# Large weights staged in tiles whose first use is late, and new instruction orders on all engines, in a two-layer attention kernel

## What is computed

```
L0: h  = x + attention(n, n)        n = rmsnorm(x), 16 heads of 16
    h  = h + attention(rmsnorm(h), ctx)
    h  = h + (silu(m @ w_gate) * (m @ w_up)) @ w_down      m = rmsnorm(h), inner 1024
L1: F  = layernorm(h); X = layernorm(ctx)
    a  = attention(F, X, X)          one head of 256, scale 1/16
    c  = gelu(a @ fc1.T + b1) @ fc2.T + b2                 inner 4
    n  = layernorm(c)
    out = F + gamma2 * (c + gamma1 * attention(n, n, n))
```

## Time and profile before

| | us |
|---|---|
| median of 3 runs (1020.12 to 1021.73) | 1021.01 |
| the profiled execution, its own time | 1021.97 |
| its span, first to last instruction | 1020.2 |
| PE busy | 899.7 (88% of the span) |
| DVE busy | 672.6 (66%) |
| ACT busy | 546.0 (54%) |
| POOL busy | 261.6 (26%) |

### The profile page before, as it was taken

How to read it: one execution, slowest core, us unless ns; L and a number is a source line. 1 busy time by engine, 2 the same in 40 slices (tenths; PEclk the granted TensorE clock), 3 DMA queues, 4 the chain that set the end, 5 groups by cost and what they waited for, 6 DMA issues and landing times.

```text
span 1020.2 us, 21920 instructions
## 1 busy us (share of the span) xinstructions
PE 899.7 (88%) x8142; PEld 762.2 (75%) x8142; DVE 672.6 (66%) x1439; ACT 546.0 (54%) x1129; POOL 261.6 (26%) x547
## 2 busy tenths in 40 slices
...
DMA packets 69266, 63.97 MB, mean 63 GB/s; under 512 B 17280, under 2 KB 64496, under 8 KB 69184
## 3 DMA queue, kind: packets, MB, share of 16 engines
q1 hardware_dynamic: 69184, 62.87, 19.3%
...
...
## 4 chain that ended last, share of the span: by engine, by line
PE 77%; DVE 12%; issue 4%; ACT 3%; DMA 2%; POOL 1%; SPq 1%; DVEq 0%; POOLq 0%; ACTq 0%
PE mring L1112 18%; PE ring L1112 17%; PE down_ps L1240 10%; PE od L1207 10%; PE ring L1193 6%; PE ring L1173 6%; DVE mx_sa L959 5%; PE ring L1120 2%; DVE xn_a L932 2%; PE mring L1345 1%; PE mring L1269 1%; PE mring L1316 1%; PE mring L1308 1%; DVE xn_m L932 1%; DVE mx_ca L964 1%
## 5 line engine op out<-in xcount | busy, mean ns | idle before, releaser
L776 ACT ACTIVATE probs<-ring 128x1024 f32<-128x1024 f32 (+1 forms) x192 | 191.8, 1020 | 42.7 <-PE ring L1193 37.5
L559 POOL TENSOR_TENSOR hidT_lo<-hid,hidT_hi 128x256 fp32r<-128x256 f32 x128 | 94.7, 749 | 377.2 <-ACT hidT_hi L799 376.7
L959 DVE TENSOR_REDUCE mx_sa<-ring 128x4 f32<-128x1024 f32 x128 | 152.8, 1218 | 13.8 <-PE ring L1173 13.5
L1008 DVE SCALAR_TENSOR_TENSOR hid<-hid,mring 128x256 f32<-128x256 f32 x128 | 53.1, 415 | 90.8 <-ACT hid L791 90.4
L1173 PE MATMUL ring<-pk_sa 63*128 63x256 f32 x512 | 61.7, 341 | 27.7 <-DVE mx_sa L959 11.8
L1240 PE MATMUL down_ps<-down_hi,hidT_hi 128*128 128x256 f32 x256 | 80.0, 312 | 0.0
L1173 PEld LDWEIGHTS ring<-pk_sa 63*128 63x128 f32 x512 | 40.3, 201 | 47.1 <-DVE mx_sa L959 15.6
L975 DVE STREAM_TRANSPOSE oS<-od 128x512 f32<-128x512 f32 x64 | 45.7, 714 | 44.5 <-PE od L1207 43.9
L1207 PE MATMUL od<-probs,vz_sa 128*32 128x256 f32 x1024 | 72.0, 400 | 1.2 <-DVE oS L975 0.5
L1240 PE MATMUL down_ps<-down_lo,hidT_hi 128*128 128x256 f32 x256 | 72.6, 284 | 0.0
L1240 PE MATMUL down_ps<-down_hi,hidT_lo 128*128 128x256 f32 x256 | 72.5, 283 | 0.0
...
## 6 DMA issues: line engine op xcount, KB each, us to landing
pk_sa<-qkT SPq DMA_DIRECT2D x96, 256.0 KB, 2.7
qpk_ca<-qkT SPq DMA_DIRECT2D x48, 256.0 KB, 2.6
x_sb<-x SPq DMA_DIRECT2D x16, 256.0 KB, 2.8
x_res<-x SPq DMA_DIRECT2D x16, 256.0 KB, 2.7
out<-o_sb SPq DMA_DIRECT2D x16, 256.0 KB, 2.2
...
```

What stands on the lines that cost most here:

```text
L559: nc.gpsimd.tensor_tensor(hidT[1][:, m % HID, :], hid[:, m % 2, :], hidT[0][:, m % HID, :].bitcast(F32), ALU.subtract).then_inc(S["hidlo"] ...
L776: nc.scalar.activation(granule(g, tag)[0:rows_, i0:i0 + 2, :, :].rearrange("p i h t -> p h i t"), ring_tile(("E", tag, k))[0:rows_].rearra ...
L959: nc.vector.tensor_reduce(mx[tag][:, :, :, k].rearrange("p q h -> p h q"), ps[:].rearrange("p h (q t) -> p h q t", t=T), AX_X, ALU.max).th ...
L1008: nc.vector.scalar_tensor_tensor(out=hid[:, m % 2, :], in0=hid[:, m % 2, :], scalar=1.0, in1=ps[:, 0:T], op0=ALU.add, op1=ALU.mult).then_i ...
```

## The change

1. `gate` is staged in a new tile `late_a`, `up` in `late_b`, and `down` in `late_a` once `gate` is split. The new tiles take the place of `h2`, `h3`, `xn_m`, `hid` (now parts of `late_a`) and of `h1`, `at`, `oS` (now parts of `late_b`), which are first written later than the staging ends. `gate` and `up` load without a wait.
2. The first exponential waits for the eight small matrices alone. Three waits are new, for the first image only: ACT's first `gu` and DVE's first `wo.ca` wait for `down` to be split, DVE's first `o.sa.0` for `up`.
3. `ORDER` is new for all engines. The numbers are shifted as well (POOL's by up to four, DVE's by one), which by itself moves nothing; the loop now starts at iteration 6 and runs seven times, where it started at 9 and ran four times.

```diff
@@ ORDER, two of its lines @@
     "pool": """
-        ms.mlp@-5 ms.ca@-4 bF@-7 lnstat.nf@-6 fold@1 pm.2@7 pm.0@18 hi.0@-5 ms.sa@-2 fs@-7 hi.1@-5 lnstat.nx@-5 hi.2@-5 hi.3@-5 hv@-6 pm.1@-2 hi.4@-5 hi.5@-5
-        xs@-6 hi.6@-5 hi.7@-5
+        xs@-3 lnstat.nx@-2 hi.6@-2 hi.7@-2 bF@-3 ms.mlp@-1 ms.ca@0 pm.0@4 lnstat.nf@-2 fs@-3 fold@1 pm.2@8 hi.0@-1 pm.1@4 hi.1@-1 ms.sa@2 hi.2@-1 hi.3@-1
+        hi.4@-1 hv@-2 hi.5@-1
@@ tiles @@
-        h1 = sb("h1", [P, QT, D])
+        QB = T // 32
+        late_a = sb("late_a", [P, 4 * QT * D])
+        h2, h3, xn_m, hid = (late_a[:, k * QT * D:(k + 1) * QT * D].rearrange("p (q d) -> p q d", q=QT) for k in range(4))
+        late_b = sb("late_b", [P, 4 * QT * D])
+        h1 = late_b[:, 0:QT * D].rearrange("p (q d) -> p q d", q=QT)
+        at = late_b[:, QT * D:2 * QT * D].rearrange("p (b c e) -> p b c e", b=QB, c=C)
+        oS = late_b[:, 2 * QT * D:].rearrange("p (c h t) -> p c h t", c=C, h=2)
@@ staging @@
-        STAGE_COL = [512 * k for k in range(8)] + [0, 2048, 0]
-        STAGE_AFTER = [0] * 8 + [4, 8, 9]
+        GATE, UP, DOWN = (W_ORDER.index(n) for n in ("gate", "up", "down"))
+        STAGE = {GATE: late_a, UP: late_b, DOWN: late_a}
 
         def stage_of(k):
-            cols = 512 if k < len(ATTN_W) else 2048
-            return probs[:].rearrange("p g i h t -> p (g i h t)")[:, STAGE_COL[k]:STAGE_COL[k] + cols]
+            if k in STAGE:
+                return STAGE[k][:]
+            return probs[:].rearrange("p g i h t -> p (g i h t)")[:, C * D * k:C * D * (k + 1)]
@@ load_w on SP @@
-                    if STAGE_AFTER[k]:
-                        sp.wait_ge(s_wlo, C * STAGE_AFTER[k])
+                    if k == DOWN:
+                        sp.wait_ge(s_wlo, C * (GATE + 1))
@@ exps on ACT @@
                 if k == 0 and at_first(n):
-                    act.wait_ge(s_wlo, C * len(W_ORDER))
+                    act.wait_ge(s_wlo, C * len(ATTN_W))
@@ gu on ACT @@
+                if m == 0 and at_first(n):
+                    act.wait_ge(s_wlo, C * (DOWN + 1))
@@ out_heads on DVE @@
+                    if tag == "sa" and at_first(n):
+                        dve.wait_ge(s_wlo, C * (UP + 1))
@@ wo on DVE @@
+                if tag == "ca" and at_first(n):
+                    dve.wait_ge(s_wlo, C * (DOWN + 1))
```

More of the change, by code:

```diff
@@ L56 @@
     "sp": """
[L57 to L58 removed]
+        wl.6@9 ldc@1 ls@8 st@-4 pqk.sa.1@1 wl.8@9 ldx@2 ldr@1 wl.3@11 mr.sa@1 ldcl@-1 wl.1@10 wl.5@10 wl.9@6 lb@7 pk.ca@0 wl.0@11 wl.10@1 wl.2@10 pq.ca@0
+        mr.ca@0 wl.7@11 wl.4@12 pqk.sa.0@2
     """,
     "pool": """
[L61 removed]
@@ L62 @@
-        xs@-6 hi.6@-5 hi.7@-5
+        xs@-3 lnstat.nx@-2 hi.6@-2 hi.7@-2 bF@-3 ms.mlp@-1 ms.ca@0 pm.0@4 lnstat.nf@-2 fs@-3 fold@1 pm.2@8 hi.0@-1 pm.1@4 hi.1@-1 ms.sa@2 hi.2@-1 hi.3@-1
+        hi.4@-1 hv@-2 hi.5@-1
     """,
     "act": """
-        hi.7@-2 aT.ca@-1 v.sa@1 nXT@-2 norm.mlp@-1 h1@0 norm.ca@0 mT2@-3 ws.5@5 ws.10@1 T.mlp@-1 v.ca@0 T.ca@0 kg@0 e2@-3 maxT.sa@1 norm.sa@2 gu.0@-1 gu.1@-1
-        qk.ca@0 hi.0@-1 E.sa.0@1 ws.7@4 gu.2@-1 hi.1@-1 E.sa.1@1 fc@4 E.sa.2@1 ws.4@6 gu.3@-1 nFT@-2 E.sa.3@1 fT@-3 E.sa.4@1 E.sa.5@1 sce@-2 ws.6@5 E.sa.6@1
@@ L67 @@
-        E.sa.7@1 pT@-2 ws.2@8 T.sa@2 hi.2@-1 hi.3@-1 maxT.ca@0 h4@-2 ws.3@7 ws.8@2 gu.4@-1 ws.0@15 qk.sa@2 cT.ca@1 gu.5@-1 E.ca.0@0 ws.9@2 hi.4@-1 hi.5@-1
-        E.ca.1@0 gu.6@-1 ws.1@13 kt@12 aT.sa@1 gu.7@-1 E.ca.2@0 E.ca.3@0 hi.6@-1 xT@-2
+        E.ca.1@-1 gu.6@-2 gu.7@-2 aT.sa@0 E.ca.2@-1 ws.8@1 E.ca.3@-1 hi.6@-2 xT@-3 hi.7@-2 v.sa@1 aT.ca@-1 mT2@-3 norm.mlp@-1 ws.5@2 e2@-3 kg@0 ws.9@1 h1@0
+        nXT@-2 norm.ca@0 T.mlp@-1 ws.3@3 v.ca@0 T.ca@0 norm.sa@2 ws.0@4 maxT.sa@1 gu.0@-1 gu.1@-1 hi.0@-1 qk.ca@0 hi.1@-1 gu.2@-1 E.sa.0@1 E.sa.1@1 E.sa.2@1
@@ L69 @@
+        E.sa.3@1 gu.3@-1 kt@1 ws.1@4 E.sa.4@1 ws.2@4 ws.6@2 nFT@-2 E.sa.5@1 fT@-3 ws.4@3 E.sa.6@1 T.sa@2 fc@1 hi.2@-1 hi.3@-1 sce@-2 pT@-2 E.sa.7@1 ws.7@2
+        gu.4@-1 maxT.ca@0 hi.4@-1 h4@-2 ws.10@1 qk.sa@2 gu.5@-1 cT.ca@1 hi.5@-1 E.ca.0@0
     """,
     "dve": """
-        ms.mlp@-2 S.sa.5@0 xn.mlp@-2 ms.ca@-1 S.sa.6@0 xn.ca@-1 T.mlp@-2 S.sa.7@0 maxsplit.sa@0 ws.1@10 T.ca@-1 lnstat.nf@-3 ws.10@0 lnstat.nx@-2 ws.5@4
-        gu.0@-2 gu.1@-2 ws.2@8 ms.sa@1 qk.ca@-1 lncen.nf@-3 u2@-4 gu.2@-2 gu.3@-2 sc@-3 o.sa.0@0 S.ca.0@-1 S.ca.1@-1 xn.sa@1 out@-4 S.ca.2@-1 S.ca.3@-1
@@ L73 @@
[L73 to L74 removed]
+        gu.5@-2 cT.ca@0 o.sa.1@0 oT.sa@0 gu.6@-2 ws.1@4 aT.sa@0 ws.3@2 ws.4@2 o.ca.0@-1 gu.7@-2 lncen.nx@-2 S.sa.0@1 S.sa.1@1 o.ca.1@-1 oT.ca@-1 wo.sa@0
+        aT.ca@-1 s2@-3 dn@-2 S.sa.2@1 wo.ca@-1 S.sa.3@1 ms.mlp@-1 ws.5@2 S.sa.4@1 xn.mlp@-1 S.sa.5@1 ms.ca@0 u2@-3 T.mlp@-1 S.sa.6@1 xn.ca@0 S.sa.7@1
```

25 lines of the change are left out of this document (8 added, 17 removed).

## The result

The change takes 1015.6 us, the median of 11 runs (1014.6 to 1017.1), beside 1021.9 before. The ratio is 0.9922, with a 95% interval of 0.9903 to 0.9942. The forecast was 1000.5: the sign is right, the size is a third of it. The profiled execution took 1015.11, its span is 1013.1.

What follows compares the result with a forecast made beforehand. PE was taken as the bound of the middle 711.7 us (busy 681.7), latency of the start. Terms -9.35 + 2.4 - 15 + 1.4 = -20.5 took 1021.97 to 1001.4; the runs' median lies 0.96 lower, so 1000.5, range 987 to 1016.

Steps and rivals of the forecast that it cites:

- Steady part: 13 middle images, mainly their score part: new orders cut PE's waits by 1.15 us per image, -15 us in all.
- The walk through the waits: One image stepped through the new orders with traced durations: PE waits 1.2 us per image in place of 2.3.
- the one on the clock: Rival: PE at work on `kg` in the second image's wait keeps later matmuls at full pace; 995.5 us, chance 0.12.
- Only the start is won: Rival: the steady part's waits move to other places, so its 15 us are not won; 1015.5 us, chance 0.17.
- The bound of -30: Best case for the 13 middle images: 30 us won, where -15 was the forecast.
- `xn_a` and `bF`: Score part: POOL's `bF` moved earlier lets DVE's `xn_a` take 0.6 us instead of 1.38, saving 0.77 us per image.
- Start: First projection of image 0 starts at 19.3 instead of 28.65 us, because small row loads come behind `gate`: -9.35 us.
- `kg`: Its 44 5-column products fill PE's 4.98 us wait in the second image, half at each clock pace: +2.4 us.
- Waits on the weights, splits, `kt` and `fc`, loop: First exponential's shorter wait, moved `gate` and `up` splits, `kt`/`fc` between exponentials, seven looped iterations instead of four: nothing each.
- End: After the last image's maxima: `lnstat.nf` behind `u2` costs about +2.9 us, faster norm products give -1.5; together +1.4.
- The gain of 1.5: At the end, two slow norm products lose `bF` beside them: -1.5 us.

Runs made afterwards that it cites:

- u2_wide: The change with `u2`'s eight 6-column products replaced by nine of 256 columns on weights, leaving out the second layer's pooled values; 999.4 us.
- bf_early: The kernel before with only POOL's `bF` moved ahead of `ms.mlp` instead of behind `ms.ca`, as in the change; 1012.5 us.
- fill_bf: The change with four added 256-column products ahead of `u2` on PE, and POOL's `bF` moved back behind `ms.ca`; 1002.5 us.
- stage_only: The kernel before with the change's new tiles, staging and waits, but all of `ORDER` from before; 1021.2 us.

## Why the forecast was right or wrong, step by step

**Steady part, -15 forecast, -5.5 measured: the step that failed.** The walk through the waits was right in total (12.2 us left; I had 1.2 us per image, 15.6). What failed is the sentence that PE "has `u2` (0.92 us, rows 9) as filling": it counts `u2` as filling that costs nothing, and puts the price in clock at nothing without a reason. The price was 12.0 us more of lost clock than before, which is more than the 9.5 by which the steady part missed. With wide products in the same stretch of time the steady part takes 693.0 us, 19 less than before (u2_wide); with `u2` itself 13.6 of these are given back. The working had no clock term in the steady part, and none of my rivals had one either; the one on the clock spoke of `kg` alone. "Only the start is won", 1015.5, has the number that came, by luck: the waits did not move to other places.

Three smaller slips in the working change no term. PE's work beside DVE's 18.6 us is not some 18.1 us; between 517.50 and 536.1 PE is busy for 16.1 and idle for 2.5. The bound of -30 gives 985.5, which the range from 987 leaves out. And the images of before are 53.3 to 56.5 us apart, not all 54.7 to 55.1.

**`xn_a` and `bF`.** Right: bf_early wins 9 to 11 us where 13 x 0.77 = 10 was the term. In the change itself `bF`'s new place is not needed for it: with `bF` back behind `ms.ca` (fill_bf) DVE's new order keeps the two apart. Whether `gu.0` ahead of `T.ca` would have covered the wait by itself, no run shows.

**Start, -9.35 forecast for the first projection, -7.75 measured.** ACT's first weight was there 1.4 us later than I counted:

```profile
9.93 1.28 ACT L704 ACT_TABLE_LOAD   x1 [9.93 <-DMA probs<-w_sa_wk]
...
20.90 0.79 PE L1118 MATMUL ring<-hT_a_hi,sa_wq_hi 128*128 128x256 f32 x2 [1.41 <-DVE hT_a_lo L939]
```

I had it third and fifth of the loads at about 8.5; the rest of the working held to 0.2 us. The first exponential starts at 51.7, where 51 was forecast.

**`kg`, +2.4 forecast.** It takes 7.73 us where 4.98 were a wait, so +2.7. Half of it at each pace was right, and in that order:

```profile
67.40 2.67 PE L1296 MATMUL down_ps<-wcT 128*128 128x5 f32 x20
69.93 5.26 PE L1296 MATMUL down_ps<-w6T 128*128 128x5 f32 x24
75.12 1.23 PE L1179 MATMUL ring<-pk_sa 63*128 63x256 f32 x8
```

The first twenty products take 0.13 us each, the others 0.22. The windows show the clock there: PE comes with a full clock, is busy without a gap with products of 5 columns, and the clock falls to half and is at half still when `kg` ends.

```profile
63.20:67.40 4.20, 4.20 (x45) 3.51 (x43) 1.04 (x3) 3.86 (x5) 0.00 (x0) 1.00 0.00 2
67.40:70.10 2.70, 2.70 (x25) 2.70 (x22) 2.63 (x6) 0.25 (x2) 0.00 (x0) 0.86 0.19 61
70.10:75.10 5.00, 5.00 (x24) 5.00 (x24) 1.62 (x3) 0.63 (x1) 0.00 (x0) 0.50 0.96 314
```

The rival that `kg` keeps the clock up fell with it. Beside it I had put a rule of the Trainium skill ("TensorE: Matmul & The Clock Gate", Part 1: activity releases the throttle). This trace does not agree with it where activity is read as busy time: the last row has PE busy for 5.00 of 5.00 us at a granted clock of 0.50.

**Waits on the weights, splits, `kt` and `fc`, loop: 0 forecast.** stage_only shows the first, 1.000. The others were not tried alone.

**End, +1.4 forecast, +4.6 measured.** The timeline of DVE, to be read against the earlier trace rows: `dn` at 977.21, then `u2`, then the statistics:

```profile
977.21 0.69 DVE L1022 TENSOR_TENSOR late_a<-late_a,down_ps 128x512 f32<-128x512 f32 x1
...
981.51 0.17 DVE L1081 RECIPROCAL rU<-mring 128x2 f32<-128x2 f32 x1 [3.61 <-PE mring L1351]
981.80 0.74 DVE L1034 BATCH_NORM_STATS2 nf_stats<-late_a 128x6 f32<-128x256 f32 x2
983.84 0.73 DVE L1049 TENSOR_SCALAR nF<-late_a,nf_mv,nf_rs 128x256 f32<-128x256 f32 x2 [0.81 <-POOL nf_rs L564]
```

The statistics start 3.9 us behind the end of `dn`, where I had about 2.9 as the whole price. The mechanism was right, its size 1.0 us short. The gain of 1.5 that I set against it does not show in the sum: of the 4.6 us, 2.8 are idle time of PE and 1.8 its busy time (121.15 to 122.94), with the granted clock at 0.83 in place of 0.86.

**Sum.** Start -6.2 (forecast -6.95), steady -5.5 (-15), end +4.6 (+1.4).
